# A graph network layer: the second message passing moved to edges sorted by receiver, summed by VectorE in SBUF

## The reference

```python
edge_dst, edge_src = (edge_index[0], edge_index[1])    # here src, dst of the graph
pre = irrep_linear(x, W_pre0, b_pre0, W_pre1)
p0, p1 = split_irreps(pre)
ip1 = einsum('eum,eum->eu', p1[edge_dst], p1[edge_src]) / 3.0
s0 = concatenate([p0[edge_dst], p0[edge_dst], ip1], axis=-1)
...
w = ssp(edge_attr @ W_f1) @ W_f2 * (ssp(s0 @ W_s1) @ W_s2)
w1, w2, w3, w4 = split(w, 4, axis=-1)
x0e, x1e = split_irreps(x[edge_src])
out0 = w1 * x0e * sh0[:, None] + w4 * (einsum('eum,em->eu', x1e, sh1) / sqrt(3.0))
out1 = w2[:, :, None] * x0e[:, :, None] * sh1[:, None, :] + w3[:, :, None] * x1e * sh0[:, None, None]
out = segment_sum(merge_irreps(out0, out1), edge_dst, N)
```

## Time and profile before

| | us |
|---|---|
| median of 3 runs | 6303.36 (6297.29 to 6304.94) |
| the profiled execution | 6299.19 |
| its span | 6297.4 |
| mean granted clock | 0.857 |

### The profile page before, as it was taken

The page is one execution under the profiler, slowest core; times in us unless marked ns, Lnnn a source line. Parts: engine busy times, 40 slices in busy tenths (PEclk is TensorE's granted clock), DMA queues, the critical chain, the costliest instruction groups (busy, mean ns, idle before and its releaser), DMA issues. The chain is left out here.

```text
span 6297.4 us, 79602 instructions
## 1 busy us (share of the span) xinstructions
PE 4863.1 (77%) x17537; PEld 2615.2 (42%) x17538; DVE 3717.9 (59%) x9258; ACT 2080.9 (33%) x4483; POOL 3133.7 (50%) x2844
## 2 busy tenths in 40 slices
PE   5545388777776888897784798888888888888797
PEld 2222155422223444454553565333334343343373
DVE  7311144477777777734235212877877787777654
ACT  1000011122222333211222102666666666666511
POOL 0677600066665666510223202777777777877500
PEclk9777588888888899898896899998888898888898
DMA  3101200055555555503534313888888888888833
GB/s 127 47 31 43 76 27 27 25 170 172 172 170 144 167 167 169 165 27 120 179 124 138 119 44 99 201 191 193 194 193 190 195 195 191 195 190 192 186 120 133
DMA packets 359491, 867.04 MB, mean 138 GB/s; under 512 B 86738, under 2 KB 109889, under 8 KB 358998
## 3 DMA queue, kind: packets, MB, share of 16 engines
q0 software_dynamic: 212464, 648.95, 42.2%
q1 hardware_dynamic: 127615, 174.83, 8.4%
q10 hardware_dynamic: 19190, 41.03, 1.7%
HBM read 643.81 MB, written 221.22 MB: 137 GB/s over the span
## 5 line engine op out<-in xcount | busy, mean ns | idle before, releaser
L766 POOL DMA_INDIRECT s_krow<-mid_att_rows,s_ix x440 | 420.4, 956 | 738.7 <-ACT s_ix L802 496.7
L1990 POOL DMA_INDIRECT mid_acc<-m_out,m_il x416 | 711.3, 1710 | 138.4 <-issue 114.5
L1977 POOL DMA_INDIRECT m_drow<-mid_drow,m_ig x416 | 457.7, 1100 | 477.7 <-DMA m_ig<-in_dst_ix 281.4
L2200 PE MATMUL m_pws<-m_w,m_hid 32*128 32x512 f32 x832 | 516.2, 703 | 202.8 <-DVE m_hid L2031 161.2
L992 PE MATMUL m_pm<-m_vrow,m_same 128*128 128x512 f32 x880 | 546.5, 710 | 150.3 <-DVE m_vrow L935 138.1
L2208 PE MATMUL m_pm<-m_msg,m_same 128*128 128x512 f32 x832 | 547.9, 745 | 133.5 <-issue 74.8
L840 PE MATMUL s_pq<-queries_q,s_same 128*128 x880 | 493.8, 699 | 110.4 <-issue 69.7
L919 POOL DMA_INDIRECT m_vrow<-mid_att_rows,m_ix x440 | 460.0, 1045 | 234.3 <-issue 127.1
L2201 PE MATMUL m_pwf<-m_w,m_hid 32*128 32x512 f32 x832 | 524.8, 713 | 0.0
L2171 PEld LDWEIGHTS m_pip<-keep_ident,m_drow 128*128 128x128 f32 x2496 | 412.9, 226 | 260.7 <-issue 254.1
L442 POOL DMA_INDIRECT mid_slots<-f_rec_now,f_row_now x416 | 419.1, 1007 | 160.8 <-issue 139.1
(11 more groups left out here) (389 smaller groups left out, 9419.4 us busy)
## 6 DMA issues: line engine op xcount, KB each, us to landing
mid_att_rows<-f_rows SPq DMA_DIRECT2D x75, 256.0 KB
mid_ys<-e_y SPq DMA_DIRECT2D x57, 256.0 KB
mid_acc<-e_zero ACTq DMA_DIRECT2D x26, 512.0 KB
g_q<-mid_qT SPq DMA_DIRECT2D x50, 256.0 KB, 4.2
g_a<-mid_acc SPq DMA_DIRECT2D x50, 256.0 KB, 3.1
mid_srow<-t_srow SPq DMA_DIRECT2D x5, 2240.0 KB
keep_w<-in_w SPq DMA_DIRECT2D x16, 512.0 KB
s_krow<-mid_att_rows,s_ix POOLq DMA_INDIRECT x440
```

Source lines behind the costliest of these rows:

```text
L766: pool.indirect_dma_start(krow[:, k % SS, :], None, io["att_rows"][1], bass.IndirectOffsetOnAxis(ap=ix[:, k:k + 1], axis=0),).then_inc(s_g ...
L1977: pool.indirect_dma_start(row, None, table, bass.IndirectOffsetOnAxis(ap=ig[:, k // EH, n, k % EH:k % EH + 1], axis=0),).then_inc(s_g[k % ...
L1990: pool.indirect_dma_start(io["acc1"][k % NACC], bass.IndirectOffsetOnAxis(ap=il[:, k // EH, k % EH:k % EH + 1], axis=0), out[:, k % R, :], ...
L2200: pe.matmul(pws[k % 2][:], hid[0:HID, par, cols], w_2[0:HID, :], start=True, stop=True)
```

## The change

`edges1` now takes the edges sorted by receiver block, as L0 does for its own:
- A second sort (`by_sender`) of the edges by `src` runs on DVE in `front0`, at nodes 10 to 19 of the first half; the table loops are unrolled. It leaves each edge's slot (`keep.row1`) and the tiles' owners (`keep.owner1`). The counting, the spreads, `leads1` and `clear_sums` go.
- An edge's record is 39 words: two gather rows, a tag, 4 values and 32 attributes. `slots1` in DRAM (128 x 440 records) is filled with empty records by 22 DMAs, which SP issues after the second half's weight loads and ahead of its node loads. POOL writes the 416 columns of records by indirect DMA, in chunks of 8 with one load each: 16 chunks in `merge0`, 7 in `gates0`, 12 in `tables1` (one behind each second residual add), 17 in `mixer1`. Each stage's POOL waits for its puts at its end. `gates0` gives up buffers: `here` and `mine` go from 10 to 4.
- `mixer1` parks X in DRAM (five DMAs of POOL, behind its 25 bias adds), DVE waits for that and clears the same 25 x 512 columns of SBUF as `keep.acc`. `merge1` reads X back, and adds `acc` and the own row only.
- `edges1` has 440 tiles in 28 bodies (the last two and the first unrolled). No scatter, no copy by ACT, no spread; records come with one SP load per four tiles; PE turns the attributes (four transposes per four tiles, ACT copies them). DVE's `add(k-2)` adds `pm` into `keep.acc` behind `message(k)`. PE's `sums(k-1)` waits for it.

The core of the diff:

```diff
+def put_chunk(pool, io, keep, rec, s_rec, s_put, first, i, count):
...
+    if i + 1 < count:
+        load(i + 1)
+    pool.wait_ge(s_rec[i % 3], 16 * (i // 3 + 1))
+    for k in range(PUT):
+        col = PUT * (first + i) + k
+        pool.indirect_dma_start(
+            io["slots1"], bass.IndirectOffsetOnAxis(ap=keep.row1[:, col:col + 1], axis=0), rec[:, i % 3, k, :], None,
+        ).then_inc(s_put[i % 3], 16)
...
 def front0
+                empty = io["slots1"].rearrange("(p t) k -> p t k", p=P)
+                for b in range(SN):
+                    sp.dma_start(empty[:, SB * b:SB * (b + 1), :], io["empty1"][:, :, :]).then_inc(s_empty1, 16)
...
+                        if n < 2 * U:
+                            order(n, by_receiver)
+                        elif n < 4 * U:
+                            if n == 2 * U:
+                                vec.wait_ge(s_k, STEPS)
+                            order(n - 2 * U, by_sender)
...
-                    vec.scalar_tensor_tensor(junk[:], pd[k // 4 % 2][:, P * (k % 4):P * (k % 4 + 1)],
-                                             keep.src[:, bass.ds(t, 1)], lower[:], ALU.is_equal, ALU.mult,
-                                             accum_out=keep.count[:, bass.ds(t, 1)]).then_inc(s_cnt, 1)
...
 def merge0
+                for i in range(PUT0):
+                    put_chunk(pool, io, keep, rec, s_rec, s_put, 0, i, PUT0)
+                all_put(pool, s_put, PUT0)
...
 def experts0
-                cleared = clear_sums(act, s_z, zero, io["acc1"], D)
...
-                act.wait_ge(s_z, cleared)
...
 def tables1
+                    pool.tensor_tensor(keep.X[:, n, :], keep.X[:, n, :], xn[:, n % U, :], ALU.add).then_inc(s_res, 1)
+                    if n % 2 == 1:
+                        put_chunk(pool, io, keep, rec, s_rec, s_put, PUT0 + PUT1, n // 2, PUT2)
+                all_put(pool, s_put, PUT2)
...
 def mixer1
+                vec.wait_ge(s_park, 16 * NB)
+                vec.memset(keep.acc[:], 0.0)
                 for c in range(KC):
...
 def edges1
-                        if there := at(b, k - 3):
-                            scatter(*there)
...
-                    vec.tensor_tensor(same[:, k // B % 2], pd[:].rearrange("p (a n) -> p a n", a=B),
-                                      keep.src[:, bass.ds(B * q, B)].unsqueeze(2).broadcast_to([P, B, P]),
-                                      ALU.is_equal).then_inc(s_same, 1)
+                    vec.tensor_tensor(same[:, par], numbers[:].unsqueeze(1).broadcast_to([P, B, P]),
+                                      loc[:, par, :].unsqueeze(2).broadcast_to([P, B, P]), ALU.is_equal).then_inc(s_same, 1)
...
-                    st.did(vec.tensor_tensor(msgs[:, 0:P], xs[:, par, 0:P], ws[:, 0:P], ALU.mult))
                     vec.wait_ge(s_st, DV * t + 2)
-                    st.did(vec.tensor_tensor(dot[:, par, :], dot[:, par, :], ws[:, 3 * P:D], ALU.mult))
+                    st.did(vec.tensor_tensor(msgs[:, 0:2 * P], x[:, 0:2 * P], ws[:, 0:2 * P], ALU.mult))
...
-                    vec.tensor_tensor(msgs[:, 0:P], msgs[:, 0:P], dot[:, par, :], ALU.add).then_inc(s_msg, 1)
...
+                def add(t, node):
+                    vec.wait_ge(s_seg, t + 1)
+                    need(vec, s_add, t)
+                    vec.tensor_tensor(keep.acc[:, node, :], keep.acc[:, node, :], pm[:], ALU.add).then_inc(s_add, 1)
...
+                        if k % B == 0:
+                            node = owners(b, k)
                         message(b, k)
+                        if at(b, k - 2):
+                            add(EU * b + k - 2, node[k % B])
                         if k % B == 2 and (there := at(b, k + 2)):
                             hidden(*there)
...
-                    act.activation(out[:, k % R, :], pm[:], ACT.Copy).then_inc(s_row, 1)
...
-                    need(pe, s_row, t)
-                    pe.matmul(pm[:], same[:, k // B % 2, k % B, :], msg[:, k % 2, :], start=True, stop=True).then_inc(s_seg, 1)
+                    need(pe, s_add, t)
+                    pe.matmul(pm[:], mine, msg[:, k % 2, P:P + D], start=True, stop=False)
+                    pe.matmul(pm[:, 0:P], mine, msg[:, k % 2, 0:P], start=False, stop=True).then_inc(s_seg, 1)
```

More of the change, by code:

```diff
@@ L538, in mix @@
                 def mix(b):
[L539 to L552 removed]
+                    mix_sums(b)
+                    mix_values(b)
+                    mix_elu(b, last_tile(b))
+                passes(vec, NT, mix)
                 vec.wait_ge(s_kv, NT)
@@ L1451, in _ @@
             def _(pool):
-                pool.memset(zero[:], 0.0).then_inc(s_zero, 1)
                 for n in range(XS):
@@ L1930, in edges1 @@
[L1930 removed]
+        s_w, s_pre, s_num = s.sem("weights"), s.sem("prepared"), s.sem("node_numbers")
+        s_rec = [s.sem(f"records{j}") for j in range(EU // B)]
         s_g = [s.sem(f"gathered{k}") for k in range(S)]
[L1932 removed]
         s_go = s.sem("go")
[L1934 to L1936 removed]
@@ L1937, in edges1 @@
-        s_go2, s_go_line = s.sem("go_scalar"), s.sem("go_line")
-        DV = 6
+        s_prod, s_ip, s_ipT, s_at, s_atT, s_h, s_soft, s_hid, s_wm, s_wf, s_w2, s_xs, s_st, s_loc, s_same, s_msg, s_seg, s_add = (
+            s.sem(n) for n in ("pair_products", "inner", "innerT", "attributes", "attributesT", "hidden_sums", "soft_steps", "hidden",
+                               "weight_products", "factors", "edge_weights", "scaled", "steps", "locals", "same", "messages", "sums",
+                               "added"))
@@ L1940, in at, with steps, bodies @@
+        s_go2 = s.sem("go_scalar")
+        DV = 5
         def at(b, k):
-            if isinstance(b, int) and not 0 <= EU * b + k < ET:
+            if isinstance(b, int) and not 0 <= EU * b + k < ST:
                 return None
             return b + k // EU, k % EU
+        def steps(b):
+            return range(ST - EU * b) if isinstance(b, int) and b == EP - 1 else range(EU)
+        def bodies(eng, body):
+            body(0)
+            with eng.Fori(1, EP - 2) as b:
+                body(b)
+            body(EP - 2)
+            body(EP - 1)
@@ L2069, in message, with owners @@
+                    ins.then_inc(s_msg, 1)
                     st.end()
+                def add(t, node):
+                    vec.wait_ge(s_seg, t + 1)
+                    need(vec, s_add, t)
+                    vec.tensor_tensor(keep.acc[:, node, :], keep.acc[:, node, :], pm[:], ALU.add).then_inc(s_add, 1)
+                def owners(b, k):
+                    _, four = nc.values_load_multi_w_load_instructions(
+                        keep.owner1[0:1, bass.ds(EU * b + k + 2, B)], engines=[mybir.EngineType.DVE], min_val=0, max_val=NT - 1,
+                        skip_runtime_bounds_check_because="each owner counts the starts of 25 blocks that a tile has reached, less one, and the first starts at 0")
+                    return four
@@ L2078, in body @@
                 def body(b):
-                    for k in range(EU):
+                    for k in steps(b):
                         if there := at(b, k + PAIR):
@@ L2144, in body @@
                 def body(b):
-                    for k in range(EU):
-                        if there := at(b, k - 2):
-                            rows(*there)
+                    for k in steps(b):
                         if k % B == 1 and (there := at(b, k + 3)):
@@ L2586, in program @@
                 run(front0)
-                run(leads1)
                 run(scores0)
```

460 lines of the change are left out of this document (187 added, 273 removed).

## The result

The changed kernel takes 7,053.91 us (median of 4 runs, 7,031.19 to 7,113.87), the kernel before beside it 6,300.32 (4 runs). The ratio is 1.122 (95% interval 1.1143 to 1.1298): slower, by 754 us, and above the range of 6,450 to 7,000. The profiled execution took 7,042.09, its span is 7,040.3.

What follows compares the result with a forecast made beforehand. POOL's three indirect DMAs a tile were taken to bound edges1, the longest stage. Terms 531 - 125 - 3 + 5 + 15 - 32 + 40 + 15 - 5 = +441 on 6,299.2 gave 6,740, then 6,745 us as median; range 6,450 to 7,000.

Steps and rivals of the forecast that it cites:

- edges1, the chain: edges1: sums wait for the add behind message, then inner, hidden and softplus; 5.9 us a tile, +531 (+400 to +640).
- the rival's condition: edges1: PE's sums, inner, hidden plus softplus fit in DVE's own step; 4.55 to 4.7 us a tile, chance 0.12.
- The clock: edges1: PE at clock 0.87 adds 0.24 us a tile to the chain.
- The puts: merge0, gates0, tables1, mixer1: 416 indirect writes of records on POOL at 1.39 us each.
- merge0: +5: merge0: bias adds and 128 puts, 210 us of POOL under a stage of 257; +5 (0 to +15).
- gates0: +15: gates0: 56 puts, 78 us under 90, and one-hot rings cut from 10 to 4; +15 (0 to +60).
- mixer1: +15: mixer1: 136 puts, 189 us under 304, and DVE's memset waiting for the parked X; +15 (0 to +60).
- the rival that they slow the stages: Stages with puts slow as front0 did, 0.44 us per us of puts; total 6,920 to 6,970 us, chance 0.14.
- the signs that I named: Signs in edges1 (waits, pitch, add), front0's second-half nodes, ACT's idle in experts0, and tables1 growing by over 120.
- tables1: tables1: 96 puts in front of the residual adds that free `xn`; +40 (0 to +120).
- front0: front0: loses counting and spreads, gains second sort and empty fills; -125 (-60 to -175).
- experts0, merge1: experts0: 26 clearing DMAs of ACT go, -32; merge1: one load of four and one add go, -5.

Runs made afterwards that it cites:

- add_start: Changed kernel with the owners' load and add(k-2) at the very start of DVE's step: 6,427.26 us, edges1 1,990.0.
- no_puts: Changed kernel with all 416 puts of records and their loads left out, only stages ahead of edges1 read: merge0 257.2, gates0 94.3, tables1 194.9, mixer1 333.7 us.
- before_paced: Kernel before with fourteen small memsets (2.9 us) on POOL behind each eight puts of front0: 6,014.68 us beside 6,345.36.
- before_twin: Kernel before, unchanged, measured on a chip of the second kind: 5,746.65 us.
- add_first: Changed kernel with DVE's add(k-2) issued ahead of message(k) in place of behind it: 6,675.83 us, edges1 2,236.2.
- after: Changed kernel, unchanged, as recorded on a chip of the first kind: 7,053.91 us median, profiled execution 7,042.09.
- after_twin: Changed kernel, unchanged, on the same chip as the kernel before's 5,746.65 us: 6,226.90 us.
- before: Kernel before, unchanged, as recorded on a chip of the first kind beside the changed kernel: 6,300.32 us.

## Why the prediction was wrong

The sign and the account of edges1 were right; that of the stages with puts was wrong, and it makes the whole miss. The span grew by 742.9 us where the sum had 441: the four stages with puts are 321 us over their terms, edges1 70 over, front0 81 under.

- *edges1, the chain:* right. +600.6 in the bounds of +400 to +640, 6.09 us a tile from the first gather to the last sums against 5.9; the wait for the softplus is 3.5 us per four tiles (said: some 3), and add_start shows the rival's condition from the other side: with the chain shorter than DVE's steps, the stage runs at DVE's own 4.52 (4.55). The repeated gap ahead of `hidden` came as said, with the one `pm` bank, but it went (1.9 us left) with the same one bank, by the place of the add. The clock was in the sum (0.24 us a tile at 0.87; it was 0.86). What I left out is that DVE's message waits for the sums of the tile before the last as well (`m_x0w`, 114.7 us over the stage, 0.26 a tile), more so where they run at half clock and take up to 1.84 + 0.42 us in place of the 1.26 laid out (granted clock 0.50 from 5,002.3 to 5,004.6 us, the message 1.19 us late at 5,004.99). The small conversions, the 256-wide multiply (417 ns) and the add (677 ns) came as worked out; the owners' load left idles of 0.2 us (said 0.4).
- *The puts:* the step that failed. "merge0: +5", "gates0: +15", "mixer1: +15" measured +158, +56 and +178, of which no_puts shows all but 2 us in gates0 and 16.5 in mixer1 to be the puts'. I took 210 us of POOL under 257 of PE as cover, since POOL and PE share no data there, and gave the rival that they slow the stages 0.14 with the words "merge0 and mixer1 are PE's, with no store for the path to wait on". What was slowed was PE's own issue. A row to doubt it by was there: in the earlier trace rows front0's window beside puts has 106 matmuls in 100 us, at a DMA share of 0.10. The rival was also priced too low, at 0.44 us per us of puts; measured were 379 / 578 = 0.66, with nearly nothing in tables1. One reason is that I compared the 106 with the stage's first 99 us (188): without the stall the same window has 246 (before_paced), which makes 0.57. Another, by my reading, is the size of the matmuls: at one in 2.8 us those of 128 columns (3.82 us for 32 without puts) lose more than front0's of 512, which came every 1.4 us. None of the signs that I named looked at merge0 or mixer1. What was late on the first kind was no transfer but PE's issue, at a DMA share of 0.12 (merge0 417), and on the second kind nothing was (merge0 258.8 with puts, 258.0 in before_twin).
- *tables1:* +40 measured +4.5. Residual adds stand between its chunks (3.4 us from the eighth put to the next), so no stall; and the wait for the adds that free `xn`, of which the term was made, did not come: DVE waits for no add of POOL there.
- *front0:* -125 measured -208.6 on the first kind and -94 on the second. The part on the counting was right: behind the puts a node of the second half takes 12.2 us (said: 12.3 to 14), where it took 19.6. The puts end 54 us later than before (825.6 against 772.0), which I had not counted. But I took none of the 25 nodes as done by then, and 8 were (64 of the 200 matmuls of L649). That is in part luck: in add_first and add_start 3 were done, and front0 took 1,077.0 and 1,073.8, some 150 below the kernel before. On the second kind front0 ends 10 us behind its last put, and that comes 45 us later than before's (819.7 against 775.2): these are the 43 us between 137 and 94.
- *experts0, merge1:* -33 and -2 (said -32 and -5).
- *Range:* the rival with 0.14 gave 6,920 to 6,970, 254 us of puts where 379 were measured; so the top of 7,000 was too low even for it (with 379 it would have read 7,049). On the second kind of chip the change costs +480, within 40 of the forecast's +441, but that is another chip than the one forecast for, and errors cancel in it: edges1 +585 (531), front0 -94 (-128), the four stages with puts +26 (75).

**Open.** What the runs of puts hold up in PE. At the 0.70 us steps the profile shows nothing that PE waits for ("issue"); written-out code suffers as looped code does (merge0 407.1 and 413.7, mixer1 497.9 and 497.7). My guess was that its instructions come late, on the first kind of chip only. No run here shows it, and the traces speak against its plain form: from 3,625 to 3,775 us the queues that the profile calls "instruction" carried three packets (q8 one, q14 two), while PE came late at nearly each of its 64 matmuls; and over the whole run they carried the same 57 and 56 packets on both kinds (after and after_twin). Why only some chips do this is open too.

## What to carry to other kernels

Ask of each instruction added to the busiest engine who waits for it and what is queued behind the waiter, and put it where the operand is ready, not where it reads well: here one add, with its owners' load, behind a message instead of at the step's start cost 700 us. Don't count a cover as free because the two engines share no data: a long unbroken run of small indirect writes cut PE's issue to a twelfth on some chips (64 matmuls in 150 us, 780 on others), and 1 us of break behind each eight of them took nearly all of that away (merge0 416.8 and 257.7, mixer1 495.0 and 338.7; 333.7 without puts). Measure a change on more than one chip before believing a term of it, with the kernel before traced on the same one.

## What the runs showed of the hardware

- Chips differ, and not in all stages. Between the two kinds the L0 gathers' stages take 685 and 567 us (scores0) and 700 and 602 (messages0), mixer1 317.2 and 317.3. In scores0 the gathers, DVE's and ACT's instructions last the same (955 and 954 ns, 686 and 685, 688 and 687); PE's are longer at the lower clock (704 and 639), and DVE waits 119.6 and 15.0 us ahead of its products with the gathered rows (530 us from 1,270 and from 940). scores0 of before and of before_twin:

```profile
1257.00:1941.00 684.00, 528.34 (x990) 185.89 (x990) 530.04 (x880) 152.78 (x264) 420.43 (x440) 0.86 0.60 169
```

```profile
926.00:1493.00 567.00, 484.10 (x990) 165.12 (x990) 539.18 (x881) 152.10 (x264) 419.96 (x440) 0.96 0.72 204
```

- On the first kind, long runs of indirect writes of 8 or 156 bytes per partition, 1.27 us apart, let PE issue one instruction per 0.70 us or a multiple, from 17 to 25 us into the run until some 10 us behind it (156 bytes; with 8 bytes the steps stand in front0's second half, and its first half stalls by whole nodes). Runs of eight with a gap of 2.1 us between them (0.9 without the break) cost nothing in merge0 (258.9 us, 257.2 without puts); runs of sixteen with a longer gap cost 50 us in mixer1 (382.9 us, 333.2 with the same break behind each eight).
- PE's granted clock was 0.86 in edges1 with the chain (busy 76%) and 0.99 with the add moved (busy 88%), for the same matmuls; the sums' lasted 813 and 645 ns on average.
